# Graph convolution: at most two indirect gathers of POOL under way at a time

## The reference

```
xn  = batchnorm(x) over the nodes                      # (6250, 64)
for every edge e:  xi = xn[dst[e]], xj = xn[src[e]]
    h   = relu([xi, xj - xi] @ W1 + b1)                # 128 hidden
    msg = h @ W2 + b2                                  # 64 out
agg = segment_max(msg, dst, 6250), 0 where a node has no edge
out = layernorm(x + relu(agg))
```

## Time and profile before

| | |
|---|---|
| median of the runs | 2434.01 us (2430.92 to 2440.19, 3 runs) |
| span of the profiled execution | 2422.7 us |
| PE busy | 1818.5 us (75%) |
| DVE busy | 1292.7 us (53%) |
| POOL busy | 1283.2 us (53%) |
| ACT busy | 862.0 us (36%) |
| gathers of b_dram | 1248, 946 ns each on POOL |
| HBM traffic | 83 GB/s over the span |

### The profile page before, as it was taken

How to read it: one execution, slowest core, us unless ns; L and a number is a source line. 1 busy time by engine, 2 the same in 40 slices (tenths; PEclk the granted TensorE clock), 3 DMA queues, 4 the chain that set the end, 5 groups by cost and what they waited for, 6 DMA issues and landing times.

```text
span 2422.7 us, 31826 instructions
## 1 busy us (share of the span) xinstructions
PE 1818.5 (75%) x12305; PEld 938.5 (39%) x12305; DVE 1292.7 (53%) x2070; ACT 862.0 (36%) x968; POOL 1283.2 (53%) x1356
## 2 busy tenths in 40 slices
PE   2046887787878778787878878878788778887785
PEld 1032444343434434343434444444444434444443
DVE  2054655565555555555555556556456555565553
ACT  2044443333333333333333333333334333333333
POOL 7715245556555565456555565555655565555621
PEclk6557899998999999898989899998999988898996
DMA  4154223233333332333323333233323333333320
GB/s 93 35 173 122 59 84 81 77 90 86 80 86 84 88 95 70 85 81 96 87 70 91 87 87 80 81 89 95 89 72 94 91 81 81 75 94 87 76 62 5
DMA packets 132832, 202.31 MB, mean 84 GB/s; under 512 B 74828, under 2 KB 76937, under 8 KB 132648
## 3 DMA queue, kind: packets, MB, share of 16 engines
q0 software_dynamic: 43440, 85.03, 16.5%
q1 hardware_dynamic: 87946, 115.04, 14.9%
q10 hardware_dynamic: 1294, 0.20, 0.1%
HBM read 189.19 MB, written 12.60 MB: 83 GB/s over the span
## 4 chain that ended last, share of the span: by engine, by line
another core or an unknown queue 38%; PE 29%; ACT 19%; issue 8%; DVE 5%; DMA 1%; SPq 0%; POOLq 0%; DVEq 0%; ACTq 0%
PE ps_g L1146 10%; PE ps_g L1153 6%; ACT hid L688 5%; ACT best L640 5%; PE ps_mr L1190 4%; ACT best L644 4%; ACT best L683 3%; PE ps_acc L1234 2%; DVE oh L919 2%; PE ps_h L1205 2%; PE ps_mr L1196 2%; PE ps_h L1215 1%; DVE runmax L993 1%; PE ps_h L1222 1%
## 5 line engine op out<-in xcount | busy, mean ns | idle before, releaser
L511 POOL DMA_INDIRECT xb<-b_dram,src_ix x1248 | 1181.1, 946 | 1031.4 <-PE ps_h L1205 384.9
L919 DVE TENSOR_SCALAR oh<-ps_k 128x1024 bf16<-128x1024 bf16 x1372 | 849.6, 678 | 1.0
L1146 PE MATMUL ps_g<-oh,xtab 128*128 128x512 bf16 x2744 | 643.5, 387 | 5.8 <-issue 5.0
L1190 PE MATMUL ps_mr<-hid,w 128*64 128x512 f32 x784 | 270.8, 776 | 369.9 <-ACT best L683 325.6
L972 DVE TENSOR_TENSOR best<-ps_acc,last_key 128x336 f32<-128x336 f32 x196 | 99.3, 507 | 815.8 <-remote 655.9
L683 ACT ACTIVATE best<-ps_mr 128x512 f32<-128x512 f32 x196 | 117.0, 597 | 1097.1 <-remote 816.3
L1146 PEld LDWEIGHTS ps_g<-oh,xtab 128*128 128x128 bf16 x2744 | 256.9, 99 | 375.6 <-issue 103.3
L1153 PE MATMUL ps_g<-oh,xtab 128*64 128x512 bf16 x2744 | 387.1, 424 | 12.6 <-issue 11.3
L993 DVE TENSOR_TENSOR_SCAN runmax<-rb,runmax,ps_mr 128x512 f32<-128x512 bf16 x196 | 249.6, 1274 | 97.4 <-PE ps_mr L1190 55.1
L688 ACT ACTIVATE hid<-ps_h,bias 128x1024 f32<-128x1024 f32 x196 | 217.9, 1112 | 106.8 <-remote 42.2
L1190 PEld LDWEIGHTS ps_mr<-hid,w 128*64 128x64 f32 x784 | 44.1, 154 | 479.6 <-ACT best L683 391.8
(11 more groups left out here) (181 smaller groups left out, 537.2 us busy)
## 6 DMA issues: line engine op xcount, KB each, us to landing
kb<-keys_dram SPq DMA_DIRECT2D x98, 504.0 KB
rb<-reset_dram SPq DMA_DIRECT2D x98, 256.0 KB
xb<-b_dram,src_ix POOLq DMA_INDIRECT x1248
src_t<-in_src SPq DMA_DIRECT2D x56, 256.0 KB
aw<-a_dram SPq DMA_DIRECT2D x196, 31.5 KB
a_dram<-oh SPq DMA_DIRECT2D x6, 672.0 KB, 3.5
xwin<-xp_dram SPq DMA_DIRECT2D x196, 10.5 KB
out<-y SPq DMA_DIRECT2D x182, 10.5 KB
```

The lines of the kernel that those rows point to most:

```text
L511: pool.indirect_dma_start(xb[:, u, t, h, :], None, b_dram[:, :], bass.IndirectOffsetOnAxis(ap=src_ix[:, b, q + t, h:h + 1], axis=0))\
L919: dve.tensor_scalar(oh[0:PN, n % NOH, :], node_keys_ps, n % TN + 0.5, None, ALU.is_equal).then_inc(oh_ready, 1)
L1146: last = pe.matmul(ps_g[:, h, :], xtab[0:PN, t, 0:2, :].rearrange("p w c -> p (w c)"), oh[0:PN, n % NOH, h * GE:(h + 1) * GE], start=t == ...
L1190: last = pe.matmul(ps_mr[h * C:(h + 1) * C, :], w2[:, :], hid[:, j % 2, h, :], start=True, stop=True)
```

## The change

The semaphores of the gathers are no longer one for each group of x and each ring slot. There are two for each of eight slots, and the gathers of a group use them in turn (n is the number of the gather in its group, n % 2 the semaphore). Both kinds of group share them, at g % NXB. Ahead of each gather POOL waits for the landing of the gather two back, in the same group or, for the first two of a group, in the one before it. PE waits on both semaphores of a group. The Else branch waits only for the last group of x, since all earlier ones have landed when it was issued.

```diff
--- before.py
+++ after.py
@@ -94,11 +94,11 @@
     def sides(k):
         return 1 if k == 0 else 2
 
-    def landed(g):
-        return 16 * TG * sides(gathered[g])
-
-    def wide_landed(i):
-        return 16 * TG * 2 * (i // NXB + 1)
+    def landed(g, n):
+        return 16 * (TG * (g // NXB) - (TG // 2 if g >= NXB and g % NXB == 0 else 0) + n // 2 + 1)
+
+    def all_landed(g):
+        return landed(g, TG * sides(gathered[g]) - 1)
 
     keys_dram = nc.dram_tensor("keys_dram", [NW, 2 * WE], bf16, kind="Internal").ap()
     reset_dram = nc.dram_tensor("reset_dram", [NW, 2 * WE], bf16, kind="Internal").ap()
@@ -273,8 +273,7 @@
         keys_out, xp_out = sem("keys_out"), sem("xp_out")
         dve_step = sem("dve_step")
 
-        rows_in = [sem(f"rows_in{u}") for u in range(NX)]
-        wide_in = [sem(f"wide_in{u}") for u in range(NXB)]
+        rows_in = [[sem(f"rows_in{u}_{p}") for p in range(2)] for u in range(NXB)]
         wide_ps = sem("wide_ps")
         key_in = [sem(f"key_in{s}") for s in range(NS)]
         rst_in = [sem(f"rst_in{s}") for s in range(NS)]
@@ -486,14 +485,22 @@
             pool.iota(part_col[:, :], pattern=[[0, 1]], base=0, channel_multiplier=1,
                       allow_small_or_imprecise_dtypes=True).then_inc(consts_ready, 1)
 
+            def one_landed_before(g, n):
+                if n >= 2:
+                    pool.wait_ge(rows_in[g % NXB][n % 2], landed(g, n - 2))
+                elif g > 0:
+                    pool.wait_ge(rows_in[(g - 1) % NXB][n % 2], all_landed(g - 1))
+
             def gather(g):
                 k = gathered[g]
                 b, q = divmod(k * TG, SB)
                 for t in range(TG):
                     for h in range(sides(k)):
+                        n = t * sides(k) + h
+                        one_landed_before(g, n)
                         pool.indirect_dma_start(xs[:, g, t, h, :], None, x[:, :],
                                                 bass.IndirectOffsetOnAxis(ap=src_ix[:, b, q + t, h:h + 1], axis=0))\
-                            .then_inc(rows_in[g], 16)
+                            .then_inc(rows_in[g % NXB][n % 2], 16)
 
             def gather_wide(i):
                 k = gathered[NX + i]
@@ -508,9 +515,11 @@
                 b, q = divmod(k * TG, SB)
                 for t in range(TG):
                     for h in range(2):
+                        n = 2 * t + h
+                        one_landed_before(NX + i, n)
                         pool.indirect_dma_start(xb[:, u, t, h, :], None, b_dram[:, :],
                                                 bass.IndirectOffsetOnAxis(ap=src_ix[:, b, q + t, h:h + 1], axis=0))\
-                            .then_inc(wide_in[u], 16)
+                            .then_inc(rows_in[(NX + i) % NXB][n % 2], 16)
 
             pool.wait_ge(src_ix_ready, 2)
             for g in range(NX):
@@ -535,8 +544,9 @@
                     pool.wait_ge(y_ready, len(GROUPS) - WB + p + 1)
                     scatter(p)
             with pool.Else():
-                for u in range(NX):
-                    pool.wait_ge(rows_in[u], landed(u))
+                for g in (NX - 1,):
+                    for p in range(2):
+                        pool.wait_ge(rows_in[g % NXB][p], all_landed(g))
 
                 def edge_tile(i, first):
                     loaded = pool.to_reg(i * 48 + 48)
@@ -1177,7 +1187,8 @@
 
                 def rows_across(k):
                     g = gathered.index(k)
-                    pe.wait_ge(rows_in[g], landed(g))
+                    for p in range(2):
+                        pe.wait_ge(rows_in[g % NXB][p], all_landed(g))
                     for t in range(TG):
                         last = pe.transpose(ps_x[:, t * P:(t + 1) * P], xs[:, g, t, :, :].rearrange("p h c -> p (h c)"), ident[:, :])
                     last.then_inc(x_ps, 1)
@@ -1199,7 +1210,8 @@
                 def rows_wide(k):
                     i = gathered.index(k) - NX
                     u = wide_slot(i)
-                    pe.wait_ge(wide_in[u], wide_landed(i))
+                    for p in range(2):
+                        pe.wait_ge(rows_in[(NX + i) % NXB][p], all_landed(NX + i))
                     for h in range(2):
                         for t in range(TG):
                             last = pe.matmul(ps_h[:, h, t * P:(t + 1) * P], xb[:, u, t, h, :], ident[:, :], is_transpose=True,
```

## The result

The changed kernel took 2448.99 us (median of 11 runs; one of them took 3401 us and is left out of the comparison), the kernel before 2434.01 us in the same job: 0.57% slower, 95% interval 0.36% to 0.78%. The forecast was 2497, 2.6% slower. Slower was the right sign, and the time lies in the range; the loss is a quarter of the forecast, and the profile shows that it came about in another way. The profiled execution has a span of 2445.9 us.

The account below looks back on a forecast made before the run. Steps were taken as bound by POOL's gather stream, which holds back PE's results, not by PE. Span 2422.7 + 57 (bursts) + 5.6 (start-up), plus 11.3 from profile to median: about 2497 us, own range 2450 to 2600, whole range 2310 to 2620.

Parts of the forecast that it names:

- the unnamed wait: ACT's copy L683, 816.3 us in 120 waits: PE's results arrive some 2.7 us after a group's last gather starts.
- A met wait costs nothing: POOL's added condition at each gather, when already met: taken as 0, other end 13 us over 1340 gathers.
- The semaphores at 0: PE waiting for two semaphores at 168 steps: taken as 0, upper bound 0.8 us a time.
- "The wait costs nothing" in quiet time: Gathers outside SP's bursts: landing and release 2.2 to 2.3 us, under two intervals of 2.50, so no cost.
- 3.0 us in a burst: Gathers beside SP's loads, once per window: 2.85 us each in place of 1.25, 2.4 gathers late, 3.0 us.
- The start-up, +5.6 us "in full": Gathers from 10 to 20 us, DMA engines fully busy: 5.6 us lost, all counted since ACT goes on after them.
- the rival's mechanism: Pauses of POOL between gathers let PE's results reach ACT at once; the faster rival, chance 0.35.
- What lies on the path: Of a burst's 3.0 us, 1.85 taken back at a group's head, 1.15 us lost in a window.
- the rival "faster": Steps in bursts fall from 11.8 towards 9.98 us as pauses let PE's results through; 2290 to 2420, chance 0.35.
- 23.0 of a window's 23.63 us: POOL's need in a window with the burst, 16 x 1.249 + 3.0, against the window's length.
- the 57 us: Wide steps' loss from SP's bursts: 50 windows at 1.15 us each.
- the sign: Whole kernel: slower 0.53, same 0.12, faster 0.35.

Follow-up runs that it names:

- cap2_x: Kernel before with the cap of two under way on the 92 gathers of x alone; 2418.00 us, 1.2% faster.
- drain4: Kernel before with one POOL wait ahead of gather 4 of each wide group until gathers 0 to 3 have landed; 2351.89 us, 3.1% faster.
- spin4: Kernel before with two POOL iotas, waiting for no landing, ahead of gather 4 of each wide group; 2359.02 us, 2.7% faster.
- gap_all_again: Kernel before with a POOL iota of 42 elements ahead of every gather, on a chip with late results; 2325.63 us, 4.7% faster.
- two_sems_no_wait: Changed kernel without the wait ahead of each gather, only waits at heads of first groups reusing a semaphore; 2448.23 us, 0.88% slower than the kernel before.
- cap2_pick31: Changed kernel with 31 picked steps in place of 28, on a chip without late results; 2403.26 us, 1.397 to the kernel before.
- gap_all: Kernel before with a POOL iota of 42 elements ahead of every gather, on a chip without late results; 2005.86 us, ratio 1.168.
- start2_drain4: Changed kernel capped only for x and the first 8 wide groups, then one wait ahead of each group's gather 4; without late results 2219.49 us, ratio 1.292.

## Why the prediction was right and wrong

**Read rightly, for one kind of chip:** the unnamed wait. Its cause was taken to be POOL's stream. ACT's 81 us beside the long stream of `cap2_x` and the shorter times with pauses (`drain4`, `spin4`, `gap_all_again`) bear this out, though no pause tried ends all of it. The same stream on the other kind holds nothing back.

**A met wait costs nothing:** shown by a gap of 0.30 at 1217.68 and, with three under way, in quiet time.

**The semaphores at 0:** wrong by 21 us in `two_sems_no_wait`, inside the bounds that I had, 0 to 0.8 us at each of 168 steps, but taken at 0 in the sum. In the changed kernel, where landings set the time, it can't be told how much of it counts.

**"The wait costs nothing" in quiet time** is the step that failed first. I took a landing as 1.9 to 2.0 us of data and 0.27 for the release, 2.2 to 2.3; the data was rightly read, but POOL goes on only at 2.76 us, 0.8 us after the last slice. The 0.27 was PE's release of POOL and not that of a DMA. The estimate of 2.15 us by the fit of the Trainium skill (page "DMA: Bandwidth & Descriptors", section on the anatomy of one DMA on the gpsimd path), with which I had the trace agree, is near the data's end and not near what a waiting engine sees; the measured 2.76 decides. At 2.76 the cap binds in every pair of gathers, 2.50 being the limit.

**3.0 us in a burst** was far too small, since it was reckoned against uncapped gathers: from 1210.55 to 1216.43 two took 5.9, and 1.785 - 1.249 over 16 gathers is 8.6 us of a window, of which quiet time's 1.39 would explain 2.3. I had 3.0 in a window, and after what is taken back 1.15, in 50 windows.

**The start-up, +5.6 us "in full":** wrong sign. With the cap ACT has its results while the gathers go on, and the eleventh scan comes 107 us sooner. I had applied the rival's mechanism to the wide steps only.

**What lies on the path:** I weighed the two mechanisms as rivals of which one would hold. Both held. Most results got through (816.3 us of unnamed waits to 188.8), as in the rival "faster"; and POOL, whose need I had put at 23.0 of a window's 23.63 us, needs 28.6 and became the bound in place of PE's results. The loss is small because the sum of capped landings, 2446 us, happens to lie beside what the late results made, 2423; the 57 us that I reckoned, bursts partly taken back at the heads of groups, are no part of it. That the sign came out right is luck.

**What no row of before could show** is that the lateness is there in some jobs, each on its own chip, and not in others. On the other kind the kernel before takes 1716 us, and the cap would cost some 43%: an estimate from the changed kernel's 2449 over 1716, since landings set it, and beside it stands `cap2_pick31`, measured at 1.397. The changed kernel itself was not run there.

Of the versions that beat both kernels where results are late (`gap_all` 4.7%, `drain4` 3.1%) `gap_all` is 17% slower on the other kind; `drain4` was not run there, but `start2_drain4` was, 29% slower. The kernel before is the best of all that ran on that kind.

## What to carry to other kernels

A cap on transfers under way limits the producer to the cap divided by a landing, and a landing must be counted as the waiting engine sees it, data, completion and restart: where cap times cadence is less than that, every item pays. Before a change trades one unnamed wait for a known one, work out the new producer's total over the whole run, not only in the burst. And where a large wait has no releaser in the profile, take the same kernel on another chip first: here the remedies for what one kind of chip does cost 11% to 40% on the other.

## What was not expected of the hardware

While POOL issued indirect gathers without a pause, PE's results came to ACT and DVE late in both profiles of the kernel before on one kind of chip (120 and 119 unnamed waits of ACT, spans of 2422.7 and 2438.8 us) and never in that on the other (0, 1713.9 us), with gathers of 946 and 947 ns and data by 1.9 to 2.0 us on both.

With a pause of 1.66 us in a group of eight gathers 74 results were still late, with one of 0.51 us at each gather 84, with one of 0.9 us in a group 109, of 120 without any. The counts don't order the times: the version with 84 gained 4.7%, that with 74 gained 2.7%. With at most two gathers under way 28 were late beside SP's full loads and 68 beside small ones.

In a long stream PE itself was slow, single matmuls 2.8 us apart, and its signals were late besides, one by 71 us (both in `cap2_x`). What holds them back no run here tells. The two kinds were met in different jobs on different chips, and no job had both, so that it is the chip and nothing else about the job is inferred from five jobs.

A gather's last data came by 2.0 us after its start, and the start of POOL that depends on it only at 2.76.
